# Routing the last batch at once: gate columns in the kept experts' order, row lists from one-hot products

## The reference, cut to what matters

```python
logits = x @ gate_weight.T                       # 128 old experts
logits = jnp.where(old_to_new[None, :] == -1, -jnp.inf, logits)
probs = jax.nn.softmax(logits, axis=-1)
top_v, top_i = jax.lax.top_k(probs, 8)
top_v = top_v / jnp.sum(top_v, axis=-1, keepdims=True)
sel_new = old_to_new[top_i]                      # 48 kept experts
flat_e, tok = sel_new.reshape(-1), jnp.repeat(jnp.arange(T), 8)
oh = (flat_e[:, None] == jnp.arange(48)[None, :]).astype(jnp.int32)
pos = jnp.sum(jnp.cumsum(oh, axis=0) * oh, axis=-1) - 1
valid = pos < 192                                # rows of one expert
# each expert: silu(gate) * up, down projection, weighted sum per token
```

## Time and profile before

| | us |
|---|---|
| median of 3 runs | 2162.82 (2157.24 to 2168.64) |
| the profiled execution | 2158.87 |
| its span, first to last instruction | 2157.1 |
| TensorE busy | 1739.3 (81%) |
| VectorE busy | 1523.6 (71%) |
| GpSimd busy | 1086.7 (50%) |
| ScalarE busy | 956.8 (44%) |
| mean granted clock of TensorE | 0.891 |

### The profile page before, as it was taken

The page is one execution under the profiler, slowest core; times in us unless marked ns, Lnnn a source line. Parts: engine busy times, 40 slices in busy tenths (PEclk is TensorE's granted clock), DMA queues, the critical chain, the costliest instruction groups (busy, mean ns, idle before and its releaser), DMA issues. The chain is left out here.

```text
span 2157.1 us, 34592 instructions
## 1 busy us (share of the span) xinstructions
PE 1739.3 (81%) x9155; PEld 1383.7 (64%) x9156; DVE 1523.6 (71%) x2883; ACT 956.8 (44%) x1867; POOL 1086.7 (50%) x817
## 2 busy tenths in 40 slices
PE   4898989347999999999998888788832079999990
PEld 3566565236888888888886555555421078888880
DVE  4477777765777888887884323788879757777774
ACT  4355452312444444444443324444423157777773
POOL 1000624564667667667676000044538657777763
PEclk9899989657999999999999898888865589999995
DMA  8011111035888888888896613131010369999967
GB/s 322 28 40 59 31 48 40 1 122 152 206 208 212 205 227 211 223 228 212 218 231 153 198 21 59 59 59 59 1 59 23 126 194 256 258 250 256 257 149 254
DMA packets 138553, 318.80 MB, mean 148 GB/s; under 512 B 30713, under 2 KB 31321, under 8 KB 136825
## 3 DMA queue, kind: packets, MB, share of 16 engines
q1 hardware_dynamic: 71448, 201.74, 27.1%
q0 software_dynamic: 64752, 112.04, 26.8%
q10 hardware_dynamic: 2288, 4.29, 0.5%
HBM read 238.68 MB, written 97.62 MB: 156 GB/s over the span
## 5 line engine op out<-in xcount | busy, mean ns | idle before, releaser
L98 POOL DMA_INDIRECT tab_rows<-pair,slot x256 | 313.7, 1226 | 452.6 <-DVEq L752 296.6
L90 PE MATMUL gu<-wgu_h,xgT_h 128*128 x648 | 233.5, 360 | 7.3 <-DVE xgT_l L1428 3.7
L1253 POOL DMA_INDIRECT xg<-x_rows,ids x167 | 191.5, 1147 | 62.5 <-issue 48.5
L90 PE MATMUL gu<-wgu_l,xgT_h 128*128 x648 | 219.6, 339 | 0.0
L90 PE MATMUL gu<-wgu_h,xgT_l 128*128 x648 | 218.3, 337 | 0.0
L1308 ACT ACTIVATE ysb<-yp,wts 128x512 f32<-128x512 f32 x160 | 110.1, 688 | 144.7 <-PE yp L1535 144.7
L90 PE MATMUL guk<-xgT_hk,wgu_hk 128*128 128x192 f32 x576 | 161.7, 281 | 0.0
L90 PE MATMUL guk<-xgT_lk,wgu_hk 128*128 128x192 f32 x576 | 158.8, 276 | 0.0
L90 PE MATMUL guk<-xgT_hk,wgu_lk 128*128 128x192 f32 x576 | 158.8, 276 | 0.0
L1298 ACT ACTIVATE sg<-gu 128x192 f32<-128x192 f32 x162 | 53.6, 331 | 235.1 <-PE gu L90 235.1
L1428 DVE TENSOR_TENSOR xgT_l<-tpx,xgT_h 128x512 fp32r<-128x512 f32 x163 | 112.2, 688 | 55.6 <-ACT xgT_h L1294 53.4
(11 more groups left out here) (503 smaller groups left out, 5043.3 us busy)
## 6 DMA issues: line engine op xcount, KB each, us to landing
wgu_sb<-in_wgu SPq DMA_DIRECT2D x64, 768.0 KB
wgu_sbk<-in_wgu SPq DMA_DIRECT2D x48, 768.0 KB, 4.4
wd_sb<-in_wd SPq DMA_DIRECT2D x64, 256.0 KB
wd_sbk<-in_wd SPq DMA_DIRECT2D x48, 256.0 KB, 5.3
ct<-in_ctxT SPq DMA_DIRECT2D x8, 1024.0 KB, 5.0
wd_sb<-in_wd SPq DMA_DIRECT2D x64, 128.0 KB
wd_sbk<-in_wd SPq DMA_DIRECT2D x48, 128.0 KB, 5.8
odd_rows<-zero SPq DMA_DIRECT2D x1, 4352.0 KB, 15.5
```

Of the source, the lines that this page charges most:

```text
L90: i = nc.tensor.matmul(out, left(k), right(k), start=(start and k == 0 and m == 0), stop=(k == ops - 1 and m == 2))
L98: nc.gpsimd.indirect_dma_start(out=tab, out_offset=bass.IndirectOffsetOnAxis(ap=s["slot"][:, n:n + 1].bitcast(U32), axis=0), in_=s["pair"] ...
L1253: nc.gpsimd.indirect_dma_start(out=xg[:, t % G, :], out_offset=None, in_=x, in_offset=bass.IndirectOffsetOnAxis(ap=ids[:, t:t + 1].bitcast ...
```

## The change

What it does, part by part:

- The gate's weights are loaded with the 128 experts on partitions, and TensorE multiplies them with the one-hot `onto` of old to new (`gate_in_new_order`), so that `gate` and `gone` have 48 columns in the new order. The indices of the maxima are then the new ones, and the mapping in `route_rows` goes.
- The drain routes its four tiles in one pass (`routed`): a one-hot `own` with experts innermost, and the mask by three additions. No scatter follows. Instead each pair's token and weight are written as bf16 parts (`parts_made`: the token number less 1792, which is exact in bf16, and the weight as three summands), `spots_made` compares each choice's position with 0 to 191, and TensorE sums spots times parts over the 32 columns into the lists of all experts. To these the lists from the first three batches' table are added (`lists_taken`).
- The table is read in the drain on SP's queue, ahead of the store of the last batch's rows, after batch 2's scatters. `ids` and `wts` live across the blocks.
- The weights of the first three kept experts are loaded in the drain's step on SP, into the buffers of `experts`; `qT` and `xT` of `mixer_two` lie in the same memory, so the loads wait for the last batch's attention.
- `xg` is cleared in four parts, and the first gathers wait for their part alone.

```diff
+def kept_weights(sp, d, s, e, gate_up, down):
+    loaded = s["kept_loaded"][e % 2]
+    if e >= 2:
+        sp.wait_ge(loaded, e // 2 * 48)
+    sp.dma_start(gate_up, d["wgu1"][e * P:(e + 1) * P, :, :]).then_inc(loaded, 16)
...
@@ kept_experts
-            for e in range(E1):
+            for e in range(NR, E1):
...
-            scatter(nc, tab, s, E1 * REG1 - 1, s_lot, BT - 1)
-
             def gather(t):
                 if t >= GK:
                     pool.wait_ge(s_xT, t - GK + 1)
+                elif t % 2 == 0:
+                    pool.wait_ge(s_clear, t // 2 + 1)
...
-            act.wait_ge(s_lot, SCAT)
-            nc.scalar.dma_start(lot[:, :, :].rearrange("t n o -> t (n o)"),
-                                tab.rearrange("(r n) o -> r (n o)", n=P)[0:T1, :]).then_inc(s_rows, 16)
...
-            nc.vector.memset(xg[:, :, :], 0.0).then_inc(s_tab, 1)
+            for n in range(NF):
+                nc.vector.memset(xg[:, 2 * n:2 * n + 2, :], 0.0).then_inc(s_clear, 1)
@@ mixer_two, SP, the drain's step
+                    else:
+                        sp.wait_ge(s_op, 2 * B * BT)
+                        for e in range(NR):
+                            kept_weights(sp, d, s, e, s["wgu"][:, e * KC:(e + 1) * KC, :], s["wd"][:, e * 2:e * 2 + 2, :])
+                        sp.wait_ge(s_scat, (B - 1) * (16 * BT * TOPK))
...
+                        sp.dma_start(lot.rearrange("t n o -> t (n o)"),
+                                     d["tab1"].rearrange("(r n) o -> r (n o)", n=P)[0:T1, :]).then_inc(s_lot, 16)
@@ POOL
-            for j in range(BT - 1):
-                pool.wait_ge(s_idx, B + j + 1)
-                settle(pool, passed)
-                scatter(nc, d["tab1"], drain, E1 * REG1 - 1, s["lot"][1], j, j + 1)
@@ route_rows
-                c.done(nc.vector.tensor_tensor(old, iota16[:, :, 0:nr], e816[:, rows].unsqueeze(1).to_broadcast([P, EOLD, nr]), ALU.is_equal))
-                c.wait()
-                c.done(nc.vector.tensor_tensor(old, old, o2nx[:, :, 0:nr], ALU.mult))
-                c.wait()
...
+                for t in (en16, en):
+                    c.done(nc.vector.tensor_copy(t[:, rows], e8[:, js[0]:js[-1] + 1, :].rearrange("p j k -> p (j k)")))
@@ drained
+                def routed():
+                    dve.wait_ge(s_lg, (B - 1) + (ROUTED + BT))
+                    routing = route_rows(c, range(BT), mm[:, :, 0:E1])
+                    next(routing)
+                    next(routing)
+                    c.done(nc.vector.tensor_tensor(own, row[:, :].unsqueeze(1).to_broadcast([P, NP, E1]),
+                                                   en16[:, :].unsqueeze(2).to_broadcast([P, NP, E1]), ALU.is_equal))
+                    c.wait()
+                    with nc.allow_low_precision("small counts"):
+                        for src, n, out in ((ours, 4, fours), (fours, 2, pairs), (pairs, 1, mask[:, :, :].unsqueeze(2))):
+                            c.done(nc.vector.tensor_tensor(out, src[:, :, 0:n, :], src[:, :, n:2 * n, :], ALU.add))
+                            c.wait()
+                    dve.sem_inc(s_mask, 1)
+
+                def parts_made():
...
+                    c.done(nc.vector.tensor_tensor(parts[:, :, 1:NV, :], own.unsqueeze(2).to_broadcast([P, NP, NV - 1, E1]),
+                                                   values[:, :, :].unsqueeze(3).to_broadcast([P, NP, NV - 1, E1]), ALU.mult))
+                    dve.wait_ge(s_lot, 16)
+                    c.done(nc.vector.tensor_copy(lotf, lot[:, :, 0]))
+
+                def spots_made():
...
+                    c.done(nc.vector.tensor_reduce(pos8[:, :], whereat, AX.X, ALU.add))
+                    c.wait()
+                    for n in range(NP):
+                        nc.vector.tensor_scalar(spots[:, n, :], places[:, :], pos8[:, n:n + 1], None, ALU.is_equal).then_inc(s_spot, 1)
...
-                for j in range(BT):
-                    route_j(j)
-                    slots_j(j)
...
+                routed()
+                parts_made()
+                spots_made()
+                lists_taken()
@@ PE
+            def gate_in_new_order():
...
+                for kc in range(KC):
+                    nc.tensor.matmul(tb[:, 0, kc * E1:(kc + 1) * E1], gate_old[:, kc * P:(kc + 1) * P], onto[:, :], start=True, stop=True)
...
+                for n in range(NP):
+                    pe.wait_ge(s_spot, n + 1)
+                    for m, (lo, w) in enumerate(((0, P), (P, IR))):
+                        nc.tensor.matmul(tb[0:w, m, 0:NV * E1].rearrange("p (v e) -> p v e", e=E1), spots[:, n, lo:lo + w],
+                                         parts[:, n, :, :], start=(n == 0), stop=(n == NP - 1))
+                nc.tensor.transpose(tp[:, 0, 0:T1], lotf, ident[0:T1, 0:T1])
+                nc.tensor.transpose(tp[:, 1, 0:T1], lot[:, :, 1].bitcast(F32), ident[0:T1, 0:T1]).then_inc(s_list, 1)
```

More of the change, by code:

```diff
@@ L2448, in route @@
                 dve.wait_ge(s_lg, b + (ROUTED + 1))
-                yield from route_rows(c, range(BT), lgp, 0)
+                yield from route_rows(c, range(BT), lgp)
                 assert c.n == KRT, c.n
@@ new lines, in lists_taken @@
+                def lists_taken():
+                    dve.wait_ge(s_list, 1)
+                    half = []
+                    for m, rows in ((0, slice(0, P)), (1, slice(0, IR))):
+                        there = tb[rows, m, 0:NV * E1].rearrange("p (v e) -> p v e", e=E1)
+                        early = [tp[rows, n, 0:T1].rearrange("p (e h) -> p e h", h=2)[:, :, m] for n in range(2)]
+                        out = [t[rows, :].rearrange("p (e h) -> p e h", h=2)[:, :, m] for t in (ids, wts)]
+                        half.append((there, early, out, idf[rows, m, 0, :], idf[rows, m, 1, :], back[rows, 0:1]))
+                    for there, _, _, f, g, b in half:
+                        c.done(nc.vector.tensor_scalar(f, there[:, 0, :], b, None, ALU.mult))
+                        c.done(nc.vector.tensor_copy(g, there[:, 3, :]))
+                    c.wait()
+                    for there, _, _, f, g, _ in half:
+                        c.done(nc.vector.tensor_tensor(f, f, there[:, 1, :], ALU.add))
+                        c.done(nc.vector.tensor_tensor(g, g, there[:, 4, :], ALU.add))
+                    c.wait()
+                    for there, early, out, f, g, _ in half:
+                        c.done(nc.vector.tensor_tensor(out[0], f, early[0], ALU.add))
+                        c.done(nc.vector.tensor_tensor(g, g, there[:, 2, :], ALU.add))
+                    c.wait()
+                    for _, early, out, _, g, _ in half:
+                        c.done(nc.vector.tensor_tensor(out[1], g, early[1], ALU.add))
+                    c.wait()
@@ L2518, in drained @@
                 scaled(3)
-                for j in range(BT):
-                    route_j(j)
-                    slots_j(j)
-                with nc.allow_low_precision("small counts"):
-                    for j in range(BT):
-                        c.done(nc.vector.tensor_tensor(s["macc1"][:, :], s["macc1"][:, :], mask[:, j, :], ALU.add))
-                        c.wait()
+                routed()
+                parts_made()
+                spots_made()
+                lists_taken()
             norm1(0, True)
-            split_folded(7, lambda ic: mm[:, ic, :], 0, -SCALE)
-            split_xT(0)
+            split_folded(6, lambda ic: mm[:, ic, :], 0, -SCALE)
             dve.wait_ge(s_w, 16 * NW)
```

251 lines of the change are left out of this document (123 added, 128 removed).

## The result

The changed kernel takes 2151.3 us (median of 20 runs, 2139.68 to 2159.59), the kernel before 2162.58 us (20 runs, 2153.35 to 2172.29). The ratio is 0.9948, 95% interval 0.9935 to 0.9961. It is faster, as forecast, but 11.3 us came where 36.8 were forecast, and 2151.3 lies above the range that ended at 2138. The profiled execution has a span of 2149.3 us, 7.8 less than the 2157.1 before.

A forecast was written before the change was run, and what follows sets the result against it. TensorE bounds the kept experts; the gap before them, ended by GpSimd's scatters, delays the first expert. Saving 27.5 us there plus 9.3 from batch 2 gives 36.8, so 2126.0 against the 2162.82 median; range 2114 to 2138.

The forecast's parts named there:

- The logits themselves cost TensorE the same, I assume.: Router logits on TensorE: 48 columns cost the same as 128, their 16 instructions taking 0.125 us each.
- the steps of batches 0 and 1 would change by 0: Second mixer's batches 0 and 1: removing the mapping is worth 0, hidden by TensorE's order of scores then positions.
- 0.2 each, 0.4 a pair ... 12 pairs at 0.4 and 20 at 0.21: 9.0.: Drain's list matmuls: low clock first, then high, 9.0 us, 9.4 with the first compare; bounds 6.4 and 12.8.
- pairs at the low clock to the end: Rival for the drain's list matmuls: 12.8 us instead of 9.0, total 2129.8; chance 0.13.
- So 13.4 us.: Hand-over from lists ready to first expert matmul: 13.4 us, ends 11.2 and 15.5.
- The experts and the tail follow unchanged.: Kept experts' loop and tail: no change in length after the first expert matmul.
- batch 2's 9.3 us: Batch 2's routing on VectorE: 9.3 us less on the path from gate columns in new order.
- the 17.6 us from logits to compares: Drain, logits to first list compare: summed as 5.6 + 8.4 + 3.6 us.
- the compares at the lower end of their bounds: Drain's 32 one-hot compares on VectorE: 0.18 to 0.33 us each, 5.8 to 10.6 us.
- no wait for the table: Drain's table read: reaches VectorE at 1684.7, about when the product ends at 1685.0; up to +3 us.
- no semaphore passed back and forth between compare and pair: Denies the mechanism of rival "Not faster": compare and pair alternate 32 times, 1.15 us more each eating 36.8; chance 0.05.
- the 6.9 named: Without early loads of experts 0 to 2, 6.9 us from last block's end to first weight cast would be exposed.

The follow-up runs named there:

- run 1: Changed kernel with the router's logits of mixer two 128 columns wide again, 80 of them zeros: 2142.21 us, ratio 0.9909 to the kernel before.
- run 2: Changed kernel with spots 256 places wide instead of 192, so both list matmuls of a pair load a 128x128 weight: 2138.74 us, ratio 0.9897.
- run 3: Changed kernel with 40 unused 128x512 matmuls put between the positions and the lists in the drain: 2140.61 us, ratio 0.9902.
- run 4: Changed kernel with weights of experts 3 and on asked for only once the first four gathers have landed: 2144.03 us, ratio 0.9924.
- run 10: Changed kernel with wide logits, one list weight shape, later loads, 40 unused matmuls, and splits begun after the first two gathers, expert 0's rows before expert 1's weights: ratio 0.9806.
- run 8: Changed kernel with weights of experts 0 to 2 asked for at the start of the kept stage, not during the drain: 2191.47 us, ratio 0.9956.
- run 5: Changed kernel with 128-column logits, one weight shape in the lists, and later loads for experts 3 and on: 2159.98 us, ratio 0.9811.
- run 6: Changed kernel with wide logits, one list weight shape, later loads, and 40 unused matmuls ahead of the lists: 2164.28 us, ratio 0.9832.
- run 7: Changed kernel with wide logits, one list weight shape, later loads, and the last three clears moved from VectorE to ScalarE: 2162.59 us, ratio 0.9833.
- run 9: Changed kernel with wide logits, one list weight shape, later loads, and only one partition row of each weight loaded from expert 4 on: 2118.83 us, ratio 0.981.

## Why the prediction was wrong

**"The logits themselves cost TensorE the same, I assume."** This step failed, and it had no range at all. At equal clock it was right (0.11 or 0.21 us a matmul at either width), but it priced the instructions and not the clock: the stretch with 48 columns per weight load ran at a lower granted clock than the one with 128, and the queries behind it started there. It cost 3.2 us in each of batches 0 and 1 and 1.6 us in the drain, and run 1 takes all of it back. That the steps of batches 0 and 1 would change by 0 was wrong for this reason alone; the missing mapping is hidden there, as forecast.

**"0.2 each, 0.4 a pair ... 12 pairs at 0.4 and 20 at 0.21: 9.0."** The second and largest failure, 12 us. The stream of 0.2 us at the low clock was right. That the weight load hides behind it was taken from the 48-column matmuls, which all load one shape; with 128 and 64 columns in turn it adds 0.10 to 0.14 us to every matmul (runs 2 and 3). And the rise of the clock was taken from the experts' unbroken stream; this one has a load between any two of its streams and stayed at 0.50 for all of its 21 us. The rival "pairs at the low clock to the end" named half of this, with 12.8 us. The upper bound should have been the sum of load and stream at the low clock, 64 times 0.33. With one shape the forecast's own course comes out: low for 5 us, then high, 9.3 us in all (run 2). The Trainium skill ("TensorEngine Tiling (Array Packing)", Restrictions) says that column tiling switches the fast weight load off. If a weight of 64 columns counts as that, which no row tells, the rows agree as far as they go: half as many columns load in 0.13 us, all 128 in 0.10. It doesn't say that the loads stop overlapping, which is most of the price.

**"So 13.4 us."** The hand-over, 17.8. Two pieces were missing. Expert 3's 1.15 MB go out together with the gathers and cost 3.8 us (run 4); the sum counted loads of experts 0 to 2 only, and not the load that the new block issues first. And the second gather takes 3.5 us beside VectorE's split; run 10, which also reorders the splits, brings the first expert matmul 1.6 us forward. The Trainium skill ("GPSIMD Engine Reference", Specifications and Key points) has GpSimd's SBUF interfaces shared with VectorE, with contention where VectorE's instruction has two SBUF inputs or runs in a two-port mode. The split has two inputs and the clear none, and rows of runs 8 and 10 show 0.98 us beside the clear and 2.47 beside the split. Not every gather that meets a split suffers: in the changed kernel the third one began 0.19 us ahead of expert 1's split and took 1.04 us.

**"The experts and the tail follow unchanged."** They got 3.7 and 5.6 us longer in the two profiles of the changed kernel. Five periods of each are over 8.5 us, waiting up to 3.1 us for gathered rows, and one or none in the two profiles of before. With the later loads the loop measured 408.8, 410.7, 411.7, 409.3 and 409.5 us (runs 4 to 7 and 10), without them 410.7, 413.1, 412.5 and 416.6 (runs 1 to 3 and 8): the excess seems to go with them, though the two groups touch. What ties a load at the start to late rows 50 to 200 us further on stays open, but the traces have a candidate. The loop's gathers of over 1.2 us, nearly all begun behind a split, are 11 and 10 in the changed kernel and one in each profile of before, where 43 begin 0.46 us ahead of a split and take 1.05 at most; they are 0 to 4 in runs 4 to 7 and 10, and 1, 6, 12 and 29 in runs 1, 2, 3 and 8, whose loops take 410.7, 413.1, 412.5 and 416.6 us. The more of them, the longer the loop, by and large (run 9, without the weights' traffic, apart). That this is the cause is argued from these counts and not shown.

**What was right:** batch 2's 9.3 us (9.4); the 17.6 us from logits to compares, with the product at 6.6; the compares at the lower end of their bounds (0.18 us each); no wait for the table; transposes 0.6 and lists 2.1; the cause for which batches 0 and 1 don't profit from the mapping; no semaphore passed back and forth between compare and pair. For a compare the prediction had 0.26 us by the Trainium skill ("VectorE: DVE Perf Modes", on the errata), which is the page's value without the factor of a perf mode by which it divides the elements; measured are 0.18. The first weights early are worth 3.9 us of hand-over (run 8), against the 6.9 named.

## What to carry to other kernels

A row in which an instruction's duration is unchanged doesn't say that a narrower one costs the same: read the granted clock over it and over what follows, for here fewer columns per weight load saved nothing and cost the next stage 1.9 us. Price a stream of matmuls as load plus stream until a row with the same sequence of weight shapes shows them overlapping, and keep the shapes equal even if columns are wasted. When a long wait is removed, list what ran unseen inside it: here weight loads and VectorE's splits met the gathers as soon as the 32 scatters were gone. And before a run that takes one load away is read as "not the limit", look whether another engine has no idle time left in it (run 9).

## What the hardware showed that I had not expected

- Thirty-two fp32 matmuls of 48 columns took 4.9 us at a clock of 0.72, the same with 128 columns 3.6 us at 1.00, in the same place (batch 1).
- Bf16 matmuls of 240 columns with weights of 128 and 64 columns in turn: 0.33 us each at the low clock, 0.21 to 0.22 at the high one. With 128 only: 0.20 and 0.10.
- A gather costs GpSimd 0.94 to 1.08 us, alone, beside clears (0.98) or begun ahead of VectorE's splits. Begun inside the first split it ends 0.2 to 0.3 us into the third, so it takes up to 2.5 us. The one that met the split 0.94 us after its own start took 3.5.
- On the second chip (runs 5 to 8) TensorE stops once for 1.9 to 3.2 us in the drain's logits, and ScalarE's copy ahead of it comes late, in all four runs, for nothing that the profile shows. The kernel before has no profile there, and the cause is open.
